# Row maxima of a latent attention: the causal mask as an extra 16-bit product, and one plain maximum over two PSUM banks

## The reference, cut to what matters

```python
c_kv = x @ Wdkv.T
q_lat = jnp.einsum('bhtd,hdl->bhtl', q, k_eff)
scores = jnp.einsum('bhtl,bsl->bhts', q_lat, c_kv) / jnp.sqrt(jnp.float32(hs))
causal = jnp.tril(jnp.ones((T, T), dtype=bool))
scores = jnp.where(causal[None, None, :, :], scores, jnp.finfo(scores.dtype).min)
attn = jax.nn.softmax(scores, axis=-1)
ctx = jnp.einsum('bhts,bsl->bhtl', attn, c_kv)
```

## Time and profile before

| | us |
|---|---|
| runs | 923.75, 926.19, 926.33 |
| median | 926.19 |
| span of the profiled execution | 923.3 |

### The profile page before, as it was taken

One profiled execution on the slowest core, in us unless ns is written; L12 is line 12 of the kernel. 1 busy time (PEld: TensorE's weight loads), 2 busy tenths in 40 slices (PEclk: granted clock), 3 DMA queues, 4 the chain that ended last, 5 costly groups with the idle time before them and its releaser, 6 DMA issues.

```text
span 923.3 us, 13156 instructions
## 1 busy us (share of the span) xinstructions
PE 832.7 (90%) x4330; PEld 534.6 (58%) x4330; DVE 766.5 (83%) x1597; ACT 605.9 (66%) x1042; POOL 430.6 (47%) x455
## 2 busy tenths in 40 slices
PE   3889999999999999989899998679788999998997
PEld 2555665665665565655565565457555555554686
DVE  3788999889989999999899998585598687876637
ACT  5677767777777676766667767374545767657531
POOL 3134354354445277787667771171323434433301
PEclk9999999999999999999999999799989999999999
DMA  3388858966977667857857668130000000000001
GB/s 122 78 184 156 143 117 190 163 126 136 206 134 153 130 131 144 166 110 144 157 103 132 136 130 159 24 106 0 1 1 1 1 0 2 0 2 1 1 1 45
DMA packets 276867, 86.29 MB, mean 93 GB/s; under 512 B 267584, under 2 KB 272448, under 8 KB 276416
## 3 DMA queue, kind: packets, MB, share of 16 engines
q1 hardware_dynamic: 275520, 80.05, 44.8%
q0 software_dynamic: 992, 5.34, 1.9%
q10 hardware_dynamic: 288, 0.07, 0.0%
HBM read 17.29 MB, written 1.05 MB: 20 GB/s over the span
## 4 chain that ended last, share of the span: by engine, by line
PE 40%; DVE 37%; issue 9%; ACT 8%; DMA 3%; POOL 1%; SPq 1%; POOLq 0%; DVEq 0%; ACTq 0%
DVE EP L1762 9%; DVE nmax L1747 8%; PE ps L1097 7%; PE ps L1099 7%; PE ps L1098 7%; PE ps L1120 4%; DVE ptm L1861 3%; PE ps L1358 3%; PE ps L1344 3%; PE ps L1135 3%; PE ps L1323 3%; DVE ps L1947 2%; DMA ET<-EP 2%; DVE OL L1821 2%; DVE st L1661 1%
## 5 line engine op out<-in xcount | busy, mean ns | idle before, releaser
L1523 ACT ACTIVATE EP<-ps,rinv 128x1024 f16<-128x1024 f32 x128 | 142.2, 1112 | 44.5 <-DVE rinv L1757 42.9
L1762 DVE SCALAR_TENSOR_TENSOR EP<-ps,rinv,EP 128x1024 f16<-128x1024 f32 x128 | 163.3, 1276 | 2.4 <-ACT EP L1523 2.0
L1513 ACT ACTIVATE ps<-ps,nmax 128x1024 f32<-128x1024 f32 x128 | 139.2, 1088 | 35.7 <-DVE nmax L1747 35.2
L1747 DVE TENSOR_REDUCE nmax<-ps 128x1 f32<-128x1024 f32 x128 | 155.0, 1211 | 0.7 <-PE ps L1099 0.7
L1097 PE MATMUL ps<-KH,QH 128*128 128x512 f32 x256 | 115.4, 451 | 8.3 <-DVE KL L1729 4.2
L2106 POOL TENSOR_TENSOR wgu<-wgu,ptm 128x688 f32<-128x688 f32 x60 | 99.7, 1661 | 45.8 <-DVE ptm L1861 43.7
L1097 PE MATMUL ps<-ET,VH 128*128 128x512 f16 x256 | 98.7, 385 | 17.8 <-DMA ET<-EP 14.2
L1099 PE MATMUL ps<-KH,QL 128*128 128x512 f32 x256 | 100.8, 394 | 0.0
L2106 POOL TENSOR_TENSOR wdn<-wdn,ptm 128x512 f32<-128x512 f32 x45 | 57.7, 1282 | 92.2 <-DVE ptm L1861 91.0
L1098 PE MATMUL ps<-KL,QH 128*128 128x512 f32 x256 | 100.5, 392 | 0.0
L1098 PE MATMUL ps<-ET,VH 128*128 128x512 f16 x256 | 98.3, 384 | 0.0
(11 more groups left out here) (250 smaller groups left out, 2126.7 us busy)
## 6 DMA issues: line engine op xcount, KB each, us to landing
wqr<-in_wqk SPq DMA_DIRECT2D x16, 256.0 KB, 3.6
wgu<-in_tern POOLq DMA_DIRECT2D x3, 1024.0 KB, 6.1
wvr<-in_wv SPq DMA_DIRECT2D x8, 256.0 KB, 3.9
wor<-in_wo SPq DMA_DIRECT2D x16, 128.0 KB, 3.1
ET<-EP SPq DMA_TRANSPOSE x128, 4.3
X<-in_x SPq DMA_DIRECT2D x2, 512.0 KB, 5.7
prw<-in_down_idx POOLq DMA_DIRECT2D x2, 256.0 KB, 7.0
tern<-in_l_wuq_rep SPq DMA_DIRECT2D x1, 512.0 KB, 4.5
```

Of the source, the lines that this page charges most:

```text
L1513: e.activation(bank, bank, ACT.Exp, bias=nmax[:, c:c + 1], scale=1.0, accum_out=rsum[:, c:c + 1]).then_inc(exped.sem, 1)
L1523: e.mul(EP[:, n % NE_RING, 0, :], SB(u, j), rinv[:, c:c + 1]).then_inc(e_hi.sem, 1)
L1747: e.tensor_reduce(nmax[:, c:c + 1], SB(u, j), AX.X, ALU.max, negate=True).then_inc(maxed.sem, 1)
L1762: e.scalar_tensor_tensor(out=EP[:, n % NE_RING, 1, :], in0=SB(u, j), scalar=rinv[:, c:c + 1], in1=EP[:, n % NE_RING, 0, :], op0=ALU.mult, ...
```

## The change: what it does

A `row_max` step is now a unit of two adjacent banks, with one semaphore for both and one release for both. For a query tile with i8 below 4 the unit holds both heads of the pair, one in each bank; for i8 from 4 on there are two units, one for each head, with keys 0 to 511 in the first bank and the rest in the second. So there are 12 units for each pair, 96 in all, with two score matmuls each as before. Where the bank holds the diagonal tile, PE adds to its 128 columns a second product, the bf16 identity by the bf16 mask tile, into the same accumulation. DVE reads both banks with one `tensor_reduce`, without a mask, and writes one or two maxima straight into `NM`; the start value `M1` is gone. `take_two` gives out the banks: if the next bank in turn is the last of the six, it is passed over. The waits of `shift` follow, and the slices of the lists are halved, so that the same query tiles stand where they stood; the costs beside the maxima are others, which shifts the places that `merge` gives them. POOL makes the two bf16 tiles in a new step `cut_mask`, and the mask that is loaded is one tile of 128 x 128.

```diff
     def maxima(p):
-        return [(0.1 + 0.001 * cuts(P * (i8 + 1))[part][1], ("row_max", 2 * p + hh, i8, part))
-                for i8 in range(8) for part in range(1 + i8 // 4) for hh in range(2)]
+        return [(0.3 + 0.002 * min(max(P * (i8 + 1), 256), 512), ("row_max", p, i8, j))
+                for i8 in range(8) for j in range(1 + i8 // 4)]
...
-        return maxima(p)[:12] + merge(maxima(p)[12:], proj(p + 1)) + second
+        return maxima(p)[:6] + merge(maxima(p)[6:], proj(p + 1)) + second
...
-    low = steps_of([f for p in (0, 1) for f in maxima(p)[:8]])
+    low = steps_of([f for p in (0, 1) for f in maxima(p)[:4]])
...
-    todo += [("point", "latent"), ("keys_zero", 2), ("stats", 2, 0, 6, 2), ("latent", 0, 0), ("stats", 2, 1, 4, 2)]
+    todo += [("point", "latent"), ("cut_mask",), ("keys_zero", 2), ("stats", 2, 0, 6, 2), ("latent", 0, 0), ("stats", 2, 1, 4, 2)]
...
-    todo += low[0:8]
+    todo += low[0:4]
...
-    todo += low[8:16]
+    todo += low[4:8]
...
-    todo += steps_of(merge([(1.0, ("values", t)) for t in range(8)], maxima(0)[8:] + shifts(0)))
+    todo += steps_of(merge([(1.0, ("values", t)) for t in range(8)], maxima(0)[4:] + shifts(0)))
...
-    todo += steps_of(merge(first[:4], merge(maxima(1)[8:], proj(2))))
+    todo += steps_of(merge(first[:4], merge(maxima(1)[4:], proj(2))))
...
+        ident16, mask16 = (sbuf(top, n, [P, P], BF16) for n in ("ident16", "mask16"))
...
-            M1 = sbuf(ctx, "M1", [P, 32])
...
-        mask = tern[:, 0, :].bitcast(F32)
+        mask = tern[:, 0, 0:256].bitcast(F32)
...
+        def take_two(step, release):
+            if count["ring"] % 6 == 5:
+                count["ring"] += 1
+            i = count["ring"] % 6
+            count["ring"] += 2
+            BANK[step] = (i, free_ring[i:i + 2])
+            free_ring[i] = free_ring[i + 1] = release
...
+            elif what == "cut_mask":
+                ident_cut.mark(0)
+                mask_cut.mark(0)
...
-                take_ring(step, row_maxed.mark(*at))
+                take_two(step, row_maxed.mark(*at))
...
-                    h, i8, part = at
-                    p, hh = h // 2, h % 2
-                    c, n = cuts(P * (i8 + 1))[part]
+                    p, i8, j = at
+                    wide = P * (i8 + 1)
                     i, freed = BANK[step]
-                    w.each([freed])
+                    w.each(freed)
                     w.wait_ge(*q_split[p, i8 // 4])
-                    w.wait_ge(*k_split(h, 0))
-                    w.wait_ge(*k_split(h, (c + n - 1) // 512))
-                    e.matmul(ps[:, i, 0:n], QT(p)[:, i8 * P:i8 * P + P], KT[p % 4][:, hh, c:c + n],
-                             start=True, stop=True).then_inc(max_scored.sem, 1)
+                    w.wait_ge(*ident_cut[0])
+                    w.wait_ge(*mask_cut[0])
+                    for k in range(2):
+                        h, c = (2 * p + k, 0) if i8 < 4 else (2 * p + j, 512 * k)
+                        n = max(min(wide - c, 512), 256)
+                        tip = wide - P - c
+                        w.wait_ge(*k_split(h, 0))
+                        w.wait_ge(*k_split(h, (c + n - 1) // 512))
+                        mm = e.matmul(ps[:, i + k, 0:n], QT(p)[:, i8 * P:i8 * P + P], KT[p % 4][:, h % 2, c:c + n],
+                                      start=True, stop=not 0 <= tip < 512)
+                        if 0 <= tip < 512:
+                            mm = e.matmul(ps[:, i + k, tip:tip + P], ident16[:, :], mask16[:, :], start=False, stop=True)
+                    mm.then_inc(max_scored.sem, 1)
...
-                        for hh in range(2):
-                            w.wait_ge(*row_maxed[2 * p + hh, i8, i8 // 4])
+                        for j in range(1 + half):
+                            w.wait_ge(*row_maxed[p, i8, j])
...
-                    h, i8, part = at
-                    p, hh, wide = h // 2, h % 2, P * (i8 + 1)
-                    c, n = cuts(wide)[part]
-                    last = part == len(cuts(wide)) - 1
-                    n = min(n, wide - c)
-                    m0, col = 1024 - wide + c, 48 + 64 * hh
-                    src = ps[:, BANK[step][0], 0:n]
-                    half = M1[:, 16 * (p % 2) + 8 * hh + i8:16 * (p % 2) + 8 * hh + i8 + 1]
-                    w.wait_ge(*max_scored[h, i8, part])
-                    w.wait_ge(*mask_in[0])
+                    p, i8, j = at
+                    wide, i = P * (i8 + 1), BANK[step][0]
+                    w.wait_ge(*max_scored[p, i8, j])
                     w.wait_ge(*zeroed["maxima_zero"])
                     if p > 1:
                         w.wait_ge(*m_turned[p - 2, 1])
-                    if part == 1:
-                        w.wait_ge(*row_maxed[h, i8, 0])
-                    e.tensor_tensor_reduce(src, src, mask[:, m0:m0 + n], 1.0, -3.0e38 if part == 0 else half,
-                                           ALU.add, ALU.max,
-                                           NM[:, p % 2, i8, col:col + 1] if last else half).then_inc(row_maxed.sem, 1)
+                    if i8 < 4:
+                        e.tensor_reduce(NM[:, p % 2, i8, 48:P:64], ps[:, i:i + 2, 0:wide], AX.X,
+                                        ALU.max).then_inc(row_maxed.sem, 1)
+                    else:
+                        src = ps[:, i:i + 2, :].rearrange("p a n -> p (a n)")[:, 0:wide]
+                        e.tensor_reduce(NM[:, p % 2, i8, 48 + 64 * j:49 + 64 * j], src, AX.X,
+                                        ALU.max).then_inc(row_maxed.sem, 1)
...
+                elif what == "cut_mask":
+                    w.wait_ge(*ident_in[0])
+                    e.tensor_copy(ident16[:, :], ident[:, :]).then_inc(ident_cut.sem, 1)
+                    w.wait_ge(*mask_in[0])
+                    e.tensor_copy(mask16[:, :], mask).then_inc(mask_cut.sem, 1)
...
-    mask = np.zeros((P, 1024), np.float32)
-    mask[:, 896:] = np.where(np.arange(P)[:, None] >= np.arange(P)[None, :], 0.0, NEG)
-    r["mask"] = mask
+    r["mask"] = np.where(np.arange(P)[:, None] >= np.arange(P)[None, :], 0.0, NEG).astype(np.float32)
```

More of the change, by code:

```diff
@@ L522, in build @@
         half_set = signal("half_set", "POOL")
+        ident_cut, mask_cut = signal("ident_cut", "POOL"), signal("mask_cut", "POOL")
         bn_stat, bn_mean, ln_var, ln_neg = (signal(n, "DVE") for n in ("bn_stat", "bn_mean", "ln_var", "ln_neg"))
```

## The result

The changed kernel takes 939.0 us (median of 4 runs, 937.8 to 940.2) against 926.3 us (the three runs listed above and a fourth of 928.7): a ratio of 1.0138, 95% interval 1.0112 to 1.0164, so 12.8 us slower. The forecast was 4.7 us faster, and the range ended at 933. The granted TensorE clock is nearly the same in both profiled executions, 0.987 before and 0.989 after, so the clock is no cause. The span of the profiled execution is 938.4 us, 15.1 us longer than before.

What follows compares the result with a forecast made beforehand. DVE was taken to set the pace in half the latent stage, PE with ACT in the other; 7.5 us gained where DVE is full less 2.8 lost elsewhere made net 4.7, so 921.5 us, range 911 to 933.

Steps and rivals of the forecast that it cites:

- What bounds the kernel: Latent block, 668 to 834 us: DVE sets the pace in half the stage, PE with ACT in the other half.
- the 19.6 us: Latent block: PE's waits for DVE to release a bank, summed over the five largest rows.
- DVE's part: Maxima of the latent block: plain two-bank maxima take about 17.8 us of work off DVE, 11.2 where it is full.
- PE's part: Score products of the latent block: 128 mask products at 0.11 us and wider 640-key rows add 15.0 us of PE work.
- the full stretches: Eight stretches of the latent block, 84 us together, with DVE busy 81.1; a gain of 7.5 us was counted there.
- The hand-over: Six-bank ring: PE needs both banks, waits up to 0.65 us longer where weights and maxima alternate; no term in the sum.
- the slower rival: Latent block: coarser hand-over and PE decide; a third of 96 units wait 0.2 us, 6.4 us; sum +9, 935; chance 0.22.
- What is free: POOL's new step, 0.6 us, fits in 1.93 us idle before zeroing KT[2]; mask load costs nothing, at most about 1 us.
- The rivals: Whole kernel: slower, 935, chance 0.22; same, 926, chance 0.18; all of DVE's saving arrives, 913, chance 0.17.

Runs made afterwards that it cites:

- b_units: cs_adjacent with both banks of a unit taken, signalled and released together, DVE still masking, no products, 640-key rows cut 512 and 128: 943.7 us, ratio 1.0198.
- d_noproduct: The changed kernel without its 128 mask products, plain maxima running over the unmasked diagonal tile too: 934.5 us, ratio 1.0097.
- j_plain_first: The kernel before, with the masked maximum over the first 512 (or 384) keys of long rows made plain, no products: 923.7 us, ratio 0.9982.
- g_release_by_bank: b_units, but each masked maximum releases its own bank and PE waits for each bank by itself; DVE still signalled once a unit: 931.4 us, ratio 1.0068.
- cs_adjacent: The kernel before in the changed kernel's order, single-bank signals and releases, units passing over the ring's last bank if they would begin there: 927.9 us, ratio 1.0031.
- f_signal_by_bank: b_units, but PE signals each bank by itself, so DVE's first masked maximum can start earlier; taking and releasing stay by unit: 942.3 us, ratio 1.0189.
- e_take_by_bank: The changed kernel, but PE waits for each bank of a unit before its own product instead of both at once: 936.3 us, ratio 1.0117.

## Why the prediction was wrong

The ladder in ratios and in us of 925.6: order 0.0003 (0.3), banks passed over 0.0028 (2.6), units 0.0167 (15.5), plain maximum -0.0101 (-9.3), products 0.0041 (3.8); sum 0.0138, 12.8 us. The rungs are differences of ratios, each uncertain by 2 to 4 us.

**What bounds the kernel.** The split into stretches where DVE is full and others was a true reading, but its conclusion was not. A full DVE is not a DVE that sets the pace alone; the stage also hangs on how early each bank comes back, as the 11.0 us of the run with five banks show. Of the 19.6 us that the text reads as waits for a bank, the 2.9 before the transposes L1333 are not: these read the maxima themselves.

**DVE's part.** Right. Of 17.8 us less work predicted, 16.9 were measured; the plain maximum over 1024 columns keeps its record of 1.22 us. Its effect on time, -9.3 us between b_units and d_noproduct, is half of the work saved. The forecast had counted 7.5. In the pipeline of single banks, j_plain_first turned 3.8 us less work into 1.7.

**PE's part.** Right in the term, a little low in the price. Two products of 256 columns start 0.24 and 0.27 us apart with a mask product between them (timeline of PE in the changed kernel), where the earlier trace rows had 0.117:

```profile
709.66 0.36 PE L1340 MATMUL ps<-KH,XH 128*128 128x256 f32 x1 [0.33 <-issue]
709.86 0.23 PE L1343 MATMUL ps<-mask,ident 128*128 128x128 bf16 x1
709.90 0.36 PE L1340 MATMUL ps<-KH,XH 128*128 128x256 f32 x1
...
710.74 0.39 PE L1340 MATMUL ps<-KH,XH 128*128 128x256 f32 x1 [0.41 <-DVE NM L1963]
710.97 0.23 PE L1343 MATMUL ps<-mask,ident 128*128 128x128 bf16 x1
711.01 0.36 PE L1340 MATMUL ps<-KH,XH 128*128 128x256 f32 x1
```

So a product adds 0.12 to 0.15 us, not 0.11, and 128 of them some 15 to 20 us of PE, an estimate from these few rows. The Trainium skill, "TensorE: Matmul & The Clock Gate", section "Back-to-back issue gap", gives about 0.081 for a matmul of 128 columns with its load; the trace does not agree for this mix. The assumption that the identity's load lies under the score product ahead did not hold in the two rows of its loads above. On the time they cost 3.2 to 3.8 us; the forecast had counted 2.8 for the part outside the full stretches.

**The hand-over.** This is the step that failed. The text described it ("PE needs both before it starts either", "what is queued behind it are the weights of the next key tile") and then left it out of the sum; only the slower rival priced it, at 6.4 us, as a third of the units by 0.2 us. It measured 15.5 us, and 2.6 more for the banks passed over, which had no price at all. Without these two the ladder's terms, 0.3 - 9.3 + 3.8, make -5.2 us, close to the forecast's -4.7. That closeness is in part luck: each term is uncertain by 2 to 4 us, and the 9.3 were gained in a pipeline that had already lost the 15.5. The claim "where several units are queued this costs nothing" is of little use, because there seldom are several: counted along the list of the changed kernel, only 18 of the 96 units follow directly on another unit, and 65 have another step of the ring on either side. The rival's price was near and its count was not: 15.5 us are 0.20 for each of the other 78 units, an estimate.

**What is free.** Right: POOL had 1.47 us left, and the mask's load lies behind that of `dq` as before.

**The rivals.** The slower one, with 0.22, had the right mechanism in its first half. Its second, that a full PE decides, is not borne out: the products cost 3.2 to 3.8 us. It gave 935, 4 us too low. The rule that `tensor_reduce` is slow, from "VectorE: DVE Perf Modes" of the Trainium skill, section "Rules for kernel authors", would have forecast a loss for the wrong reason: DVE's 16.9 us less work and the 9.3 us between b_units and d_noproduct show the swap itself to be a gain.

What stays open: g_release_by_bank is still 0.0037 above cs_adjacent (3.4 us), which may be DVE's later start together with the other cut of the 640-key rows; f_signal_by_bank tests the first only while the release is late. Taking and releasing by the bank were changed together there, and e_take_by_bank shows only that taking alone gives little. What the swap would give with each bank released by itself is open: one instruction over two banks can't do that.

## What to carry to other kernels

Where several engines share a ring of buffers and walk one list in order, price a change of grain first: join two buffers into one unit and each waits for the other, which here cost 15.5 us while the cheaper instruction that it made possible gave 9.3. A quick test of how much a stage depends on its depth is to take one buffer away, which cost 11.0 us here; where it costs that much, a step that holds a buffer longer for a faster instruction must pay for it in the sum. A wait that the prediction describes must have a number in its sum.

## What the runs showed of the hardware

By the records, the 16-bit weight load of the identity was mostly not pulled under the score product ahead of it: in 88 of 128 cases PE's weight side stood about 0.2 us before it, 17.4 us in all, with no releaser shown ("issue" in the waits above). In both rows shown, at 705.66 and 708.06, the load starts together with its own product.

In the timeline of the 256-column products, the next score product starts only 0.04 us after the mask product, but 0.24 to 0.27 us after the score product before it, where the plain pitch was 0.117. So the records of single matmuls don't give what a product costs; the distance between its neighbours does.
